# New written-out instruction sequences for all five engines of a fused decoder layer on one core

## What is computed

```
x = layernorm(x + attn(x))           # linear attention with a memory M, z; q, k, v of 128
x = layernorm(x + xattn(ctx, ctx, x))# long convolution over 512 features, heads of 8
x = layernorm(x + ffn(x))            # gate/up and down weights in packed FP4, silu, rms norm

attn:  q, k, v = x Wq, x Wk, x Wv;  s(.) = elu(.) + 1
       memory = s(q) M / (s(q) z + eps)
       local  = sum over earlier tokens of (s(q) . s(k)) v / (s(q) . cumsum s(k) + eps)
       out    = (g memory + (1 - g) local) Wo
xattn: kv[i, j] = k[i] v[j] within a head; y = causal convolution of kv with ssm_kernel, + kv D
       out[j] = sum over i of y[i, j] q[i]
ffn:   h = silu(x Wgate) * (x Wup);  y = h Wdown;  y / sqrt(mean(y*y) + eps)
```

## Time and profile before

| | |
|---|---|
| median of three runs | 536.75 us (536.4 to 536.91) |
| span of the profiled execution | 535.3 us |
| its own time | not recorded apart from the runs; the median is 1.45 us above the span |
| busy: TensorE, its weight loads | 508.7 us (95%), 377.6 us (71%) |
| busy: VectorE, ScalarE, POOL | 374.4 us (70%), 415.7 us (78%), 394.7 us (74%) |
| granted TensorE clock, mean | 0.995 |
| DMA | 40.6 MB, 29.6% of the 16 engines' span |
| a period in the loop | 51.2 us |

### The profile page before, as it was taken

How to read it: one execution, slowest core, us unless ns; L and a number is a source line. 1 busy time by engine, 2 the same in 40 slices (tenths; PEclk the granted TensorE clock), 3 DMA queues, 4 the chain that set the end, 5 groups by cost and what they waited for, 6 DMA issues and landing times.

```text
span 535.3 us, 11768 instructions
## 1 busy us (share of the span) xinstructions
PE 508.7 (95%) x3676; PEld 377.6 (71%) x3676; DVE 374.4 (70%) x1145; ACT 415.7 (78%) x994; POOL 394.7 (74%) x449
## 2 busy tenths in 40 slices
...
GB/s 224 203 39 63 169 142 180 128 80 99 87 112 24 159 127 86 23 100 79 60 1 117 59 59 0 118 59 59 13 130 14 39 33 49 0 1 42 1 21 39
DMA packets 66146, 40.63 MB, mean 76 GB/s; under 512 B 37882, under 2 KB 55418, under 8 KB 66106
## 3 DMA queue, kind: packets, MB, share of 16 engines
q1 hardware_dynamic: 66106, 40.13, 29.6%
...
## 4 chain that ended last, share of the span: by engine, by line
PE 36%; POOL 27%; issue 19%; ACT 5%; DVE 4%; SPq 4%; DMA 2%; POOLq 1%; DVEq 0%; ACTq 0%
POOL shared L297 9%; POOL h_lo L1102 5%; SPq L415 4%; POOL kv L197 3%; PE p_cv L137 3%; PE p_cv L139 3%; PE p_cv L138 3%; PE p_n L1299 3%; PE p_n L1297 3%; PE p_n L1298 3%; POOL shared L299 2%; PE p_x L1284 2%; PE p_x L1286 2%; PE p_qk L1284 2%; PE p_qk L1286 2%
## 5 line engine op out<-in xcount | busy, mean ns | idle before, releaser
L1102 POOL TENSOR_TENSOR h_lo<-w,h_hi 128x256 f16<-128x256 f32 x88 | 73.6, 842 | 44.6 <-ACT h_hi L1151 43.0
L137 PE MATMUL p_cv<-kv_hi,toe 128*128 128x288 f16 x320 | 91.6, 286 | 1.3 <-DVE shared L257 1.3
L139 PE MATMUL p_cv<-kv_hi,toe 128*128 128x288 f16 x320 | 91.5, 286 | 0.0
L138 PE MATMUL p_cv<-kv_lo,toe 128*128 128x288 f16 x320 | 91.5, 286 | 0.0
L1134 ACT ACTIVATE p_qk<-p_qk,rescale 128x256 f32<-128x256 f32 x192 | 78.3, 451 | 12.5 <-PE p_qk L1286 11.9
L297 POOL TENSOR_TENSOR shared<-shared 128x1024 f32<-128x1024 f32 x32 | 76.8, 2399 | 8.9 <-DVE shared L257 8.8
L1134 ACT ACTIVATE p_x<-p_x,rescale 128x256 f32<-128x256 f32 x192 | 78.4, 452 | 6.2 <-PE p_x L1286 6.0
L1134 ACT ACTIVATE p_s<-p_s,rescale 128x256 f32<-128x256 f32 x144 | 59.0, 456 | 11.2 <-PE p_s L1286 11.1
L1297 PE MATMUL p_n<-wd_hi,h_hi 128*128 128x512 f16 x176 | 66.8, 379 | 0.0
L1298 PE MATMUL p_n<-wd_lo,h_hi 128*128 128x512 f16 x176 | 66.7, 379 | 0.0
L1299 PE MATMUL p_n<-wd_hi,h_lo 128*128 128x512 f16 x176 | 66.7, 379 | 0.0
...
## 6 DMA issues: line engine op xcount, KB each, us to landing
...
```

Of the source, the lines that this page charges most:

```text
L137: nc.tensor.matmul(dst, hi, kh, start=(mb == 0), stop=False)
L138: nc.tensor.matmul(dst, hi, kl, start=False, stop=False)
L139: done = nc.tensor.matmul(dst, lo, kh, start=False, stop=(mb == lb))
L1102: nc.gpsimd.tensor_tensor(h_lo[:, i, :], h32[:, i % 2, :], h_hi[:, i, :], ALU.subtract).then_inc(h_low, 1)
```

## The change

All twelve sequences are written anew. The multiset of steps of every sequence is the same as before; only their order differs. Two waits are added: ScalarE's `deviations(i)` waits for its own earlier ones, and VectorE's `add_residual` waits for the `finish` that read `z3` before.

```diff
         def deviations(i):
             act.wait_ge(mean_made, i + 1)
+            wait(act, deviated, 2 * i)
             for e in range(2):
...
         def add_residual(f, t):
             dve.wait_ge(rr_made[t], f + 1)
             dve.wait_ge(cv.x2_held[t], f + 1)
+            wait(dve, fin_made[t], f)
             if isinstance(f, int) and f == 0:
...
-    START_SYNC = ("x3 x4 cx2 st0 cx3 tw0 x5 st1 st2 x6 st3 toe0 xq0 xq2 toe1 xq1 x7 cx5 cx4 xr1 xr0 toe2 st4 cx6 xq3 "
+    START_SYNC = ("x3 cx2 cx3 x4 st0 tw0 x5 st1 toe0 cx4 x6 st2 st3 xq0 xq2 toe1 x7 cx5 xq1 toe2 xr1 xq3 xr0 "
...
-    PE_ORDER = ("y1_0 g0_0 g1_0 y1_1 g0_1 y1_2 ct0 g1_1 g0_2 y1_3 y1_4 g2_0 g0_3 c2 g1_2 g3_0 c3 y1_5 g2_1 g1_3 g3_1 "
+    PE_ORDER = ("y1_0 y1_1 g0_0 g1_0 y1_2 g2_0 g0_1 y1_3 g1_1 g2_1 g0_2 y1_4 g1_2 g0_3 y1_5 c2 c3 g2_2 y1_6 "
...
-    LAST_ACT = ("ho0 rs0_1 rs1_1 rs2_1 tl rs0_2 rs1_2 rs0_3 rs2_2 rs1_3 gu0 rs2_3 hh0 gu1 rs3_1 gu2 rs4_1 rs3_2 hh1 "
+    LAST_ACT = ("rs0_1 rs1_1 rs2_1 rs0_2 rs1_2 rs2_2 rs0_3 tl rs1_3 rs2_3 gu0 gu1 hh0 hh1 gu2 rs3_1 rs4_1 "
```

More of the change, by code:

```diff
@@ L1338, in decoder_layer @@
     x1_blocks = nc.dram_tensor("x1_blocks", [2 * NG, 4, P, P], F32, kind="Internal").ap()
-    START_SYNC = ("x3 x4 cx2 st0 cx3 tw0 x5 st1 st2 x6 st3 toe0 xq0 xq2 toe1 xq1 x7 cx5 cx4 xr1 xr0 toe2 st4 cx6 xq3 "
-                  "xr2 toe3 xq5 xr3 st5 toe4 xq4 cx7 st6 toe5 st7").split()
-    START_PE = ("ze0 Xa0 iw0 iw1 iw2 Xb0 iw3 Q0 iz0 V0 S0 Xa1 M0 N0 Xb1 w0 w1 Q1 T0 w2 f0 w3 Oa0 Ob0 Xa2 S1 V1 w4 w5 "
[8 rows of a table removed]
-                "+y0_6 +xt0 +d0 +y0_7 +y0_8 +y0_9 +xt1 +y0_10 +d1").split()
-    START_DVE = ("ze0 is0 u0 sg0 mk0 ig0 dn0 fs0 o0 u1 sg1 ra0 rb0 bm0 mk1 u2 dn1 bn0 o1 kl0 nb0 sg2 ra1 rb1 bm1 mk2 "
[6 rows of a table removed]
-                 "+xt0 +xt1 +a0 +b0 +e0").split()
@@ L1359, in decoder_layer @@
-    START_ACT = ("xa0 kw0 kw1 xb0 kw2 kw3 re0 ge0 vk0 ks0 xa1 xb1 lc0 rv0 wh0 wh1 re1 ok0 kt0 wh2 rv1 wh3 qs0 xa2 vk1 "
[8 rows of a table removed]
[L1368 to L1372, removed]
@@ L1374, in decoder_layer @@
-    PE_ORDER = ("y1_0 g0_0 g1_0 y1_1 g0_1 y1_2 ct0 g1_1 g0_2 y1_3 y1_4 g2_0 g0_3 c2 g1_2 g3_0 c3 y1_5 g2_1 g1_3 g3_1 "
[3 rows of a table removed]
[L1378 to L1382, removed]
-                 "rs7_1 hh5 kn rs6_3 rs7_2 rs8_1 ct1 rs7_3 rs8_2 gu6 gu7 rs8_3 hh6 rs9_1 rs10_1 rs9_2 ho1 rs10_2 rs9_3 "
-                 "hh7 gu8 rs10_3 gu9 hh8 gu10 hh9 xt0 hh10 xt1 n0").split()
@@ L1385, in decoder_layer @@
-    POOL_ORDER = ("pr1 hl0 pr2 tr0 hl1 pr3 tr1 hl2 hl3 pn a1 hl4 hl5 tr2 tr3 hl6 bn0 b1 hl7 bn1 hl8 hl9 hl10 a0 b0").split()
-    LAST_PE = ("y1_0 y1_1 y1_2 g0_0 g1_0 g2_0 g0_1 g1_1 y1_3 y1_4 g0_2 g2_1 g1_2 y1_5 g0_3 g2_2 g1_3 y1_6 g3_0 g2_3 "
-               "g4_0 g3_1 y1_7 g5_0 y1_8 g4_1 y1_9 g3_2 y0_0 g5_1 g4_2 y1_10 g3_3 g5_2 y0_1 g4_3 y0_2 g6_0 g5_3 g6_1 "
-               "g7_0 y0_3 g6_2 g8_0 g7_1 g6_3 y0_4 g7_2 w1_0 g8_1 g9_0 w1_1 g7_3 y0_5 w1_2 g10_0 g8_2 w1_3 g9_1 "
-               "g10_1 g8_3 g9_2 w1_4 g10_2 w1_5 g9_3 w1_6 g10_3 w1_7 y0_6 w1_8 w1_9 w1_10 y0_7 y0_8 y0_9 y0_10").split()
@@ L1391, in decoder_layer @@
-    LAST_DVE = ("gu0 gu1 gu2 a1 gu3 gu4 gu5 b1 gu6 gu7 gu8 e1 gu9 gu10 A1 B1 a0 b0 E1 e0").split()
-    LAST_ACT = ("ho0 rs0_1 rs1_1 rs2_1 tl rs0_2 rs1_2 rs0_3 rs2_2 rs1_3 gu0 rs2_3 hh0 gu1 rs3_1 gu2 rs4_1 rs3_2 hh1 "
-                "hh2 rs5_1 rs4_2 rs3_3 rs5_2 rs4_3 n1 gu3 rs5_3 hh3 gu4 rs6_1 gu5 hh4 rs6_2 rs7_1 rs6_3 rs7_2 rs8_1 "
-                "gu6 hh5 rs7_3 hh6 rs9_1 gu7 rs8_2 hh7 rs10_1 rs8_3 rs9_2 rs10_2 gu8 rs9_3 rs10_3 hh8 gu9 gu10 hh9 "
-                "hh10 ho1 N1 n0").split()
-    LAST_POOL = ("hl0 hl1 hl2 a1 hl3 hl4 hl5 b1 hl6 hl7 hl8 hl9 hl10 A1 a0 B1 b0").split()
+    START_SYNC = ("x3 cx2 cx3 x4 st0 tw0 x5 st1 toe0 cx4 x6 st2 st3 xq0 xq2 toe1 x7 cx5 xq1 toe2 xr1 xq3 xr0 "
+                  "xr2 toe3 toe4 xq4 xq5 xr3 toe5 cx6 cx7 st4 st5 st7 st6").split()
@@ new lines, in decoder_layer @@
+    START_PE = ("ze0 iw0 iw1 Xa0 Xb0 iz0 iw2 iw3 Q0 V0 Xa1 S0 w0 Xb1 M0 N0 Q1 T0 Xa2 Oa0 w1 Ob0 w2 f0 w3 V1 "
[9 rows of a table added]
+                "+g10_3 +xt0 +y0_6 +y0_7 +y0_8 +y0_9 +xt1 +y0_10").split()
+    START_DVE = ("ze0 is0 fs0 u0 sg0 ig0 mk0 dn0 sk0 o0 u1 ra0 rb0 sg1 mk1 bm0 dn1 u2 o1 ra1 rb1 bm1 sg2 bn0 "
[7 rows of a table added]
+                 "+b0 +e0 +kq1").split()
+    START_ACT = ("kw0 kw1 xa0 xb0 ks0 kw2 kw3 re0 vk0 ge0 xa1 xb1 rv0 lc0 wh0 ok0 wh1 re1 kt0 rv1 vk1 xa2 "
[9 rows of a table added]
+                 "+hh10 nm6 +xt1 +n0 nm7").split()
```

21 lines of the change are left out of this document (added), and 56 rows, old and new, of tables (LAST_PE, PE_ORDER, START_ACT, START_DVE).

## The result

The changed kernel takes 534.95 us, the median of five runs (534.7 to 535.32), against 536.75 of before: ratio 0.9966, 95% interval 0.9954 to 0.9978. That is 1.8 us or 0.34% faster, beyond the 0.2% that a measurement can tell, and 0.25 us from the forecast of 535.2. The profiled execution took 535.32 us, with a span of 533.6 where before had 535.3.

What follows compares the result with a forecast made beforehand. TensorE was taken to bound the loop, SyncE's queue and then POOL's sums the first stage. Terms +1.2 − 0.7 − 0.3 − 1.7 = −1.5 gave span 533.8, time 535.2 us; forecast's own range 533.7 to 536.7, with rivals 531.6 to 540.0.

Steps and rivals of the forecast that it cites:

- The first stage: Start of the kernel: c2 4.5 us later, 2.6 us more TensorE work done, so 1.2 us lost; bounds −3.6 and +4.5.
- period 7: Period 7 has the same heads as the full periods: 0.3 us won.
- the full periods: Periods 2 to 6: some 0.15 of 0.4 us a period won, together −0.7 us; bounds −2.0 and +1.5.
- period 8: Last period: rescales first, hold of x2 near the end; −1.7 us, bounds −2.5 and +0.5.
- idles some 6 us: First stage: TensorE comes to c2 near 87, no later than before, and waits there while c2 starts at 93.4.
- the count of what comes back: First stage: period 1's c2 and c3, 21 matmuls or 2.6 us, fill TensorE's former 2.7 us idle before the first gate step.
- Rival A: First stage: SyncE's queue decides, the late xq passes on in full; 537.8 us, or 540.5 with slower issues; chance 0.22.
- Rival B: First stage: meetings of VectorE's kv_lo with POOL's sums end, POOL chain 3.6 us shorter; 531.6 us; chance 0.15.
- The relief by keeping VectorE and POOL apart: In the loop, ending the clashes of VectorE and POOL is worth nothing, since neither engine is the bound there.
- near edges: Full periods: four steps with under 0.1 us to spare (g0_3, g8_2, g9_1, c12), and tm15 late by 0.1.
- 0.4 us bound on the loop: Loop: TensorE's work is 50.8 us a period, so 0.4 us is all a new sequence can take out.
- Rival C: Loop: two near edges late by 0.2 us, a period 0.4 longer than forecast, +2.0 in all; 537.2 us; chance 0.10.

Runs made afterwards that it cites:

- fill_the_wait: Changed kernel with TensorE kept busy in its wait: six matmuls ahead of T5 and two behind it, results unread; 533.13 us, ratio 0.9939.
- vector_pool_order_only: Kernel before with only VectorE's and POOL's loop sequences from the changed kernel; 573.05 us, ratio 1.0668.
- tensor_order_only: Kernel before with only TensorE's loop steps y1_1, y1_3 and y1_5 moved ahead of g0_0, g0_2 and c2; 536.7 us, ratio 0.9992.
- new_loop_only: Kernel before with the four loop sequences of the changed one, start and last sequences as before; 535.14 us, ratio 0.9960.

## Why the prediction came out right

The number was right within 0.3 us, and that was partly luck. The first stage came out 1.4 us worse than its term, period 7 and the full periods together 1.4 us better; only period 8 was right in both cause and size.

**The first stage, predicted +1.2, measured +2.6.** The queue and VectorE's order went as written: slot 0 stored at 46.2, `xq` there at 90.7 (forecast 90.0: the issue of a store took 6.6, 8.9, 8.9 and 7.7 us for slots 0 to 3 where 7.6 was taken, and the load of `xq` took 2.7 us instead of 3.7), terms 0 at 93.09, c2 at 94.1 (93.4). The step that failed is the sentence that TensorE "idles some 6 us", priced as idle time alone. It idled, lost its clock, and ran c2, c3 and Oa5 at half speed, which with the 0.7 us of c2 put POOL's sums at 100.4 and not at 97.2. `fill_the_wait` shows the price: 2.6 us in its trace, 1.5 to 1.8 by ratios and medians. Without it period 2 would have started where it did before (176.13 against 176.10), so the rest of the term was too dear by 1.2. That lies in the count of what comes back. The prediction counted c2 and c3 of period 1, 2.6 us. By the same count of stalls, period 1 had 3.20 us of them behind g0_0 before and has 1.41 now, 1.8 us that no term contained (0.63 behind g0_3 and behind g9_0 were the largest). With c2 0.7 us later than forecast this gives the 1.2: 1.8 less 0.7, to a tenth. The stores of slots 4 to 7 cost nothing, as forecast: slot 4's began at 165.7 and took 11.7 us to issue, and period 2 has 0.10 us of stalls.

**Rival A** did not decide: c2 and c3 of period 1 did run ahead of g0_0 without a wait for their terms, and with the clock kept the 5.2 us of delay at c2 are all recovered by period 2. So its threshold, 2.6 us of added delay at c2, was too low. One of its signs did appear: g0_0 started at 134.29, past 132, but without the gap before it. **Rival B** did not happen: two sums at L299 and one at L304 still met `kv_lo`, and the chain of sums takes 26.6 us as before (100.39 to 127.03, against 92.74 to 119.40). The relief by keeping VectorE and POOL apart was argued to be worth nothing in the loop. In the changed kernel a loop period's four `kv_lo` take 1.36 to 1.72 us, where before they took 1.36 to 2.05, and the 0.28 us of the period are all in TensorE's stalls. `vector_pool_order_only` has them at 1.34 to 1.42, but its period is longer by other waits. No run isolates the relief alone with ScalarE's order fitting it, so what it is worth stays open. The Trainium skill, page "SBUF — State Buffer", section "Who interferes with whom", has a VectorE instruction with two SBUF inputs and a GpSimd instruction that reads SBUF exclude each other. The two `kv_lo` of that run that meet nothing, 1.34 and 1.35 us, and the L299 that meets one, 2.28 us for 1.27, agree.

**Full periods, predicted −0.7, measured −1.1.** A period went from 51.20 to 50.92, 0.28 instead of 0.15; the fifth of them, the unrolled period 2, had nothing to give (stalls 0.04 before, 0.10 after). Of the near edges that kept 0.25 us back in the forecast, only g8_2 shows a wait in the trace, 0.10 us; the stalls left are 0.12 us a period. So the 0.4 us bound on the loop held, and the part taken was mis-sized. Rival C, for the same reason, did not happen. But the two runs with a down step put first and `tensor_order_only` show how little it needed: each single move traded the gap at g0_0 for one at g0_1 or rt1, and the period came to 51.47 or 51.17. What is shown is that the four loop sequences together gain (`new_loop_only`) and that three partial edits of TensorE's, and VectorE's with POOL's, do not. TensorE's whole new sequence alone, or any set of three, was not run.

**Period 7, predicted −0.3, measured −1.3.** Its stalls went from 1.37 to 0.03. The forecast took only the gap at its start; period 7's other stalls, 1.0 us, were not looked at one by one.

**Period 8, predicted −1.7, measured −1.7.** Its stalls fell from 2.56 to 0.85, `ho0` being 1.15 of it.

Together: +2.6 − 1.1 − 1.3 − 1.7 = −1.5 at y0_10, and −1.7 in the span, where the forecast was −1.5. The 1.45 us that the forecast added to the span came out as 1.35 (534.95 against 533.6).
